# Each engine's loop starts at the first slot of an instruction block

## The reference

```python
x = _layernorm(x + _L0_attn_ref(x, Wq, bq, Wk, bk, Wv, bv, Wo, bo))
x = _layernorm(x + _L0_xattn_ref(x, ctx_2048, ctx_2048, Wi, bi, Wf, bf, ln_scale))
x = _layernorm(x + _L0_ffn_ref(x, select_weight, ..., bias_w, debias_w))
```

## Time and profile before

| what | value |
|---|---|
| time, median of 3 runs | 1926.44 us (1921.48 to 1927.14) |
| span of the profiled execution, first to last instruction | 1919.0 us |
| PE busy, share of the span | 1766.6 us, 92% |
| DVE, ACT, POOL busy | 81%, 41%, 40% |
| instruction packets | 42 on queue 8, 17 on queue 14 |

### The profile page before, as it was taken

The page is one execution under the profiler, slowest core; times in us unless marked ns, Lnnn a source line. Parts: engine busy times, 40 slices in busy tenths (PEclk is TensorE's granted clock), DMA queues, the critical chain, the costliest instruction groups (busy, mean ns, idle before and its releaser), DMA issues.

```text
span 1919.0 us, 67339 instructions
## 1 busy us (share of the span) xinstructions
PE 1766.6 (92%) x27529; PEld 1464.6 (76%) x27656; DVE 1557.8 (81%) x3898; ACT 783.8 (41%) x2193; POOL 759.3 (40%) x779
## 2 busy tenths in 40 slices
PE   0889999999999999999999999999999999999985
PEld 0678787887887788788778778878877877887863
DVE  4456888888888888888888888888888888888876
ACT  2134344434434434443443444444344344444431
POOL 1034344334434433433443443343344344334333
PEclk9999999999999999999999999999999999999985
DMA  4112222221221222222122222222212222222110
GB/s 138 60 58 75 70 67 84 78 82 60 82 77 66 80 75 67 79 81 78 63 80 77 66 82 73 69 77 82 77 66 77 77 66 82 74 76 69 66 57 28
DMA packets 53829, 141.14 MB, mean 74 GB/s; under 512 B 8767, under 2 KB 10431, under 8 KB 45578
## 3 DMA queue, kind: packets, MB, share of 16 engines
q1 hardware_dynamic: 53770, 140.31, 21.4%
HBM read 122.98 MB, written 17.30 MB: 73 GB/s over the span
## 4 chain that ended last, share of the span: by engine, by line
PE 83%; DVE 6%; ACT 6%; issue 3%; SPq 1%; POOL 0%; DMA 0%; POOLq 0%; ACTq 0%; DVEq 0%
PE bank L493 12%; PE bank L365 10%; PE bank L366 9%; PE bank L368 9%; PE bank L347 8%; PE bank L355 4%; PE quad L481 4%; PE bank L448 4%; PE bank L460 3%; PE bank L507 3%; PE bank L360 3%; PE bank L356 3%; PE bank L519 3%; PE bank L462 3%; ACT x_high L584 2%
## 5 line engine op out<-in xcount | busy, mean ns | idle before, releaser
L734 POOL TENSOR_TENSOR ex<-ex,w_rec 128x512 f32<-128x512 f32 x64 | 67.2, 1050 | 766.4 <-DVE w_rec L848 766.4
L642 ACT ACTIVATE Dx<-Mb,a_col 128x128 f32<-128x128 f32 x1024 | 313.0, 397 | 0.0
L493 PEld LDWEIGHTS bank<-c,Dx 128*128 128x128 f32 x2048 | 244.4, 192 | 30.1 <-ACT LT L672 21.6
L493 PE MATMUL bank<-c,Dx 128*128 128x33 f32 x2048 | 246.7, 276 | 17.1 <-ACT LT L672 14.7
L746 POOL TENSOR_TENSOR h_rs<-h_ve,half_neg 128x16 f32<-128x16 f32 x64 | 186.9, 2921 | 147.1 <-DVE h_ve L934 147.1
L615 ACT ACTIVATE x1T<-bank 128x512 f32<-128x512 f32 x64 | 38.3, 598 | 357.8 <-PE bank L347 357.8
L913 DVE SCALAR_TENSOR_TENSOR Dx<-quad,Dx 128x512 f32<-128x512 f32 x256 | 159.0, 683 | 11.5 <-PE quad L481 2.8
L760 POOL TENSOR_TENSOR rs<-ve,half_neg 128x1 f32<-128x1 f32 x192 | 106.1, 553 | 155.0 <-DVE ve L869 154.9
L739 POOL TENSOR_SCALAR_AFFINE_SELECT Dx<-Dx 128x512 f32<-128x512 f32 x256 | 159.8, 637 | 5.4 <-ACT Dx L642 5.4
L594 ACT ACTIVATE ex<-ex 128x512 f32<-128x512 f32 x64 | 40.3, 630 | 239.3 <-DVE ex L839 239.3
L347 PE MATMUL bank<-id_sb,x 128*128 128x128 f32 x512 | 85.7, 291 | 54.9 <-DVE x2sq L954 53.0
(11 more groups left out here) (157 smaller groups left out, 4351.5 us busy)
## 6 DMA issues: line engine op xcount, KB each, us to landing
Mb<-m_rows SPq DMA_DIRECT2D x64, 1024.0 KB, 4.6
xb<-in_x SPq DMA_DIRECT2D x256, 64.0 KB
xr<-in_x SPq DMA_DIRECT2D x64, 256.0 KB, 2.6
cb<-in_ctx SPq DMA_DIRECT2D x64, 256.0 KB, 3.5
out_dram<-yo SPq DMA_DIRECT2D x64, 256.0 KB, 2.4
Dx<-in_wq SPq DMA_DIRECT2D x4, 256.0 KB, 4.5
Dx<-in_wk SPq DMA_DIRECT2D x4, 256.0 KB, 5.5
Mb<-in_wv SPq DMA_DIRECT2D x4, 256.0 KB, 5.6
```

What stands on the lines that cost most here:

```text
L493: last = mm(bank[6 + h // 8][:, (h % 8) * HD:(h % 8 + 1) * HD], Dx[t.parity()][:, h % 4, h // 4, :], c1[:, h, :], start=True, stop=True)
L642: last = go(Dx[t.parity()][:, j, n, :], Mb[t.parity()][:, h, :], ACT.Exp, bias=a_col[t.parity()][:, h:h + 1], scale=-1.0)
```

## The change

The loop is no longer opened with `eng.Fori` but with the same function underneath it, which gets one more argument: for this engine the loop's first instruction is to be loaded at slot 0 of an instruction block of 256 slots (16 KB). The slots between the code ahead of the loop and that place are left unused, and the engine passes them with one taken branch when it enters the loop. `eng.Fori` gave the same engine and bounds. All five engines open their loop here. The operations, their order and their waits stay the same, ahead of the loop, in it and behind it.

```diff
         def steps(eng, step, stop=NT):
             for k in range(PEEL):
                 step(Tile(k))
-            with eng.Fori(PEEL // 2, stop // 2) as u:
+            with nc.Fori(PEEL // 2, stop // 2, engines=[eng.engine], head_slot={eng.engine: 0}) as u:
                 regs = {k: eng.snap(u * 2 + k) for k in range(-LAGS - 2, 3)}
```

## The result

The changed kernel takes 1933.39 us (median of 20 runs, 1923.92 to 1940.79), the kernel before 1922.65 us on the same chips (20 runs, 1918.07 to 1928.85): a ratio of 1.0049, 95% interval 1.0036 to 1.0062, or 9.4 us (6.9 to 11.9) more. The time lies in the predicted range and the direction is right. The size is not: the forecast was 4.15 us, and 9.4 us lies just above the rival with the clock drop (7.4 to 9.1 us). Slower by over 0.3% came, which had 0.26.

A forecast was written before the change was run, and what follows sets the result against it. The prediction had TensorE (PE) busiest, 92% of a 1919.0 us span. Loop 0, PE entry 1.45, behind it 1.6 and tail 1.1 sum to 4.15 us, taking 1926.4 to 1930.5 us, range 1924 to 1936.

The forecast's parts named there:

- the rival with the clock drop: At PE's entry: jump discards the fetch, 3.0 us paid, half clock follows; 7.4 to 9.1 us in all, chance 0.24.
- Slower by over 0.3%: Whole kernel: an outcome slower by more than about 5.8 us, what the measurement can tell from no change; chance 0.26.
- The loop, 0: Loop body: no instruction added, same number of resident blocks, so 0 us; bounds 0 and a gain of 6.2 us.
- a cheaper way back: Jump to the loop's first instruction becomes free on DVE and PE: 1920 to 1922 us, rival's chance 0.04.
- The entry on PE, +1.45: PE's jump into the loop: waits for the next block, still being fetched, 1.4 to 1.6 us; bounds 0 and 2.1.
- Behind the entry, +1.6: Just after the loop's entry: the larger of two waits lying beside each other, 1.6 us; bounds 0 and 2.6.
- (b): DVE's loop entry: target block not the one being fetched, 2.4 us late, leaving PE 1.6 us of wait at VT.
- (a): PE's second loop block, needed 3.1 us behind the head in L415: a wait of 0 to 0.5 us.
- The tail, +1.1: PE's code behind the loop: next block boundary at the end of L415 comes too soon, 1.1 us; bounds 0 and 1.3.
- its dearest case, 9.9 us: Upper end of the range: 2.1 + 2.6 + 0.5 + 1.3 + 3.4 = 9.9 us, leading to 1936 us.

The follow-up runs named there:

- the second placed version: Against the kernel before: all five loops aligned, PE's at slot 28, and PE, ACT, POOL and DVE shifted at their starts; 1914.91 us, ratio 0.9944.
- PE alone: Against the kernel before: only PE's loop head put at slot 0, the other four engines open their loop as before; 1930.27 us, ratio 1.0043.
- the head at slot 28: As the changed kernel with all loops aligned, but PE's loop head at slot 28; 1927.61 us, ratio 1.0029 to the kernel before.
- the others alone: Against the kernel before: the other four engines' loops at slot 0, PE's loop as before; 1930.85 us, ratio 1.0044.
- The tail alone: Against the kernel before: loops stay, only PE's code behind its loop moved to the change's slot by a taken branch; 1933.49 us, ratio 1.005.
- DVE late: Against the kernel before: no alignment, one memset of an unused tile ahead of DVE's loop; 1928.58 us, ratio 1.0031.
- PE placed: Against the kernel before: only PE's stream shifted at its start to slot 246 and its loop head at slot 28; 1915.09 us, ratio 0.9957.

## Why the prediction was right in kind and too small

**The loop, 0: right.** Tiles of 28.18 against 28.19 us, no instruction packet from 365 to 1836 us, PE's and DVE's busy times in the loop as before. The possible gain from a cheaper way back did not come (its price was also added up wrongly: 6.2 us less 0 to 4 us leads to 1920 to 1924 us, not 1922). The aligned loop is neither faster nor slower in itself: the second placed version aligns all five and the first only PE's, at the same time.

**The entry on PE, +1.45: right,** 1.68 measured (idle 1.61, forecast 1.4 to 1.6). The block was being fetched when the jump came: its packet began at 308.80 us, ahead of L514, and took 0.96 us (59.9% of 1.6), L460 followed 1.5 us behind its end, and no second packet came in between. So the jump did not start the fetch anew, or the idle would have been nearer 3.0 us. PE alone and the head at slot 28 had 1.86 and 1.78 us, somewhat more than forecast. On DVE, where the target was not the block being fetched, the idle of 2.73 us is a whole fetch (2.4 us late was forecast). The Trainium skill, "Runtime: NRT & Kernel Launch", section "Instruction fetch mechanics", has a taken branch outside the resident blocks force a fetch; DVE's trace agrees, PE's paid only its remainder. The same section of the Trainium skill calls crossings mostly hidden; the 1.64 us in L415 is one that is not.

**Behind the entry, +1.6: right,** 1.54 for VT and 0.27 at L471, 1.92 in all. It was DVE (b). The second block (a) showed no wait in the changed kernel, and one of 0.73 us with the head at slot 28, more than the 0 to 0.5 that I gave it. PE alone aligned has no wait for VT, the others alone have exactly this one.

**The tail, +1.1: the step that failed.** "Bounds 0 and 1.3" was too low for the wait itself, 1.64 us: it was read from one stall, whose packet took 1.11 us, and this one's took 1.65 (103.4% of 1.6). And "The code behind that is slow and sparse" left out what follows: the dense matmuls of the next step, 5.45 us of them, which ran at half the clock and lost 4.7 us. So this term was 6.6 us by these rows (8.14 with the end) instead of 1.1. The tail alone gives 9.6 us, with a dearer wait. The sum put the loss to the clock behind any wait at nothing; that is the larger part of what was missing.

**The clock.** The rival was right that the clock would follow a stall, and its sum of 7.4 to 9.1 us is the nearest to what came. Its place, its size and its condition were wrong. I had it behind the entry, where the changed kernel's profile shows 1.00; a stretch was to be 3.41 us, and at the loop's edges 10.24 us came in three of the profiles, 13.66 in one; and it was to need an idle of some 2 us. It came behind idles of 1.64 (the change), 1.87 (PE alone), 1.54 (DVE late) and 1.70 us (PE placed), and did not come behind 1.61 (the change, entry), 1.86 (PE alone, entry) and 1.54 (the others alone). Ahead of the loop it came in the changed kernel behind a still shorter one, 1.8 us before the stretch at 196.87 us:

```profile
195.11 0.25 PE L415 MATMUL quad<-KT,QT 32*32 32x32 f32 x5 [1.21 <-issue]
```

What decides between them, no run here shows.

**The timed runs.** Every timed run of the experiments has its span and its mean granted clock on record. An estimate of what the low clock took from a run is its span times (1 - clock), that is half of the time at 1.2 GHz, as if PE had been busy throughout. The means against the kernel before on the same chip, in us (for the whole change, against all 73 runs of the kernel before in the experiments, as those on its own chips have no clock on record):

| kernel | span | by the clock | rest |
|---|---|---|---|
| the whole change | +8.4 | +4.3 | +4.2 |
| PE alone | +7.7 | +4.8 | +2.9 |
| the others alone | +7.2 | +7.5 | -0.2 |
| DVE late | +5.6 | +3.1 | +2.5 |
| the tail alone | +10.3 | +8.4 | +1.8 |
| PE placed | -8.2 | -6.8 | -1.4 |

The 95% intervals are 1 to 2 us wide to either side for the rest and 2 to 4 us for the others, so that for DVE late alone the clock's share is not clear of nothing. The rest of the whole change, 4.2 us (3.1 to 5.2), lies at the forecast of 4.15; what the forecast left out is the clock.

**Luck.** The forecast stood on a median of three runs, 1926.44 us, where 20 runs give 1922.65. On the latter the sum would have led to 1926.8 us and its dearest case, 9.9 us, to 1932.6, below what was measured. That the time fell into the range, and only 2.9 us from the forecast, is in part owed to a start that was 3.8 us too high.

**What stays open.** The parts do not add up. PE alone +8.3, the others alone +8.4, and together +9.4, where the sum would be 16.7, outside the interval. By the table the rest does add within its intervals (2.9 - 0.2 against 4.2) and the clock's share does not (4.8 + 7.5 against 4.3). Each profile with the half clock at the loop's edges has one stretch there, whether it has one wait or three; that the parts share one such loss would fit this, but where the timed runs had their half clock is not on record, and the profile of the others alone has none at the loop's edges, so this is argued and not shown. The late entries of ACT, POOL and SP were not tried apart from DVE's.

## What to carry to other kernels

Aligning a loop's head to a block gives nothing by itself; what counts is whether the loop stays within the blocks that the engine holds (seven here, with eight it took 107 us more), and how long before the jump, or before the next boundary in a dense run of small operations, the present block was entered. Move the code so that the loop is entered late in a block and no boundary in dense code is reached less than some 3 us behind the one before (in the tail the next block came 3.2 us after the first L409): that gave 0.9957 here without a changed operation. And price a stall of the bounding engine with the clock that may follow: one wait of 1.54 us cost 6.0 and 8.4 us in these runs, two to four waits of 2.5 to 5 us in all 5.5 to 9.6 us.

## What was not expected of the hardware

The same kernel, run again, had stretches at half clock of other lengths (3.41 us in one execution, 10.24 in another), and its loop started 4.2 us later. A loop one block too long was charged not one fetch in each iteration but about 4.5 (117 packets in 26 iterations), in bursts of up to nine in one, with whole iterations free of them. A 1.54 us wait that had nothing to do with code, made by a late operation of another engine, cost as much in the runs as the same wait behind code that came late (6.0 and 8.4 us, with intervals that overlap).
